# Two self-attentions with their exponentials taken head by head

## What is computed

```
scores = jnp.einsum('bhqd,bhkd->bhqk', q, k) / jnp.sqrt(HEAD_DIM)
scores = jnp.where(causal, scores, -jnp.inf)      # layer 2
attn = jax.nn.softmax(scores, axis=-1)
out = jnp.einsum('bhqk,bhkd->bhqd', attn, v)
```

## Time and profile before

| | us |
|---|---|
| median of 3 runs | 2552.9 |
| lowest and highest run | 2545.34, 2553.57 |
| profiled execution | 2537.7 |
| its span | 2535.8 |
| exponentials of layer 1, first to last start | 743.5 to 966.0 |
| exponentials of layer 2, first to last start | 1782.1 to 1990.2 |

### The profile page before, as it was taken

One profiled execution on the slowest core, in us unless ns is written; L12 is line 12 of the kernel. 1 busy time (PEld: TensorE's weight loads), 2 busy tenths in 40 slices (PEclk: granted clock), 3 DMA queues, 4 the chain that ended last, 5 costly groups with the idle time before them and its releaser, 6 DMA issues. The chain is left out here.

```text
span 2535.8 us, 36942 instructions
## 1 busy us (share of the span) xinstructions
PE 2066.5 (81%) x12688; PEld 1249.8 (49%) x12688; DVE 1552.3 (61%) x3620; ACT 1175.2 (46%) x2304; POOL 762.3 (30%) x938
## 2 busy tenths in 40 slices
PE   5874996768748888997889889775899898677898
PEld 4663662225612324664444444463334466566755
DVE  5867348989848884555554545354567444745676
ACT  3443437644436664224767666533345422133445
POOL 0420005543331100002655555442644100044213
PEclk8985997988959998998999999876789899698899
DMA  1000000000042200002323322102121000200000
GB/s 46 31 7 1 1 1 6 1 28 27 1 117 47 47 2 1 1 1 89 84 72 80 84 71 72 56 1 46 43 55 31 1 1 18 81 1 1 1 1 18
DMA packets 39034, 80.36 MB, mean 32 GB/s; under 512 B 7392, under 2 KB 21728, under 8 KB 37952
## 3 DMA queue, kind: packets, MB, share of 16 engines
q1 hardware_dynamic: 36384, 75.00, 11.1%
q10 hardware_dynamic: 2464, 2.99, 0.5%
HBM read 51.75 MB, written 7.34 MB: 23 GB/s over the span
## 5 line engine op out<-in xcount | busy, mean ns | idle before, releaser
L740 ACT ACTIVATE spt<-P 128x1024 f32<-128x1024 f32 (+3 forms) x256 | 220.9, 863 | 186.0 <-PE P L594 186.0
L707 DVE TENSOR_REDUCE smf<-P 128x2 f32<-128x1024 f32 (+3 forms) x256 | 254.5, 1020 | 47.4 <-PE P L583 24.1
L2274 PEld LDWEIGHTS P<-W,e_h 128*128 128x128 f32 (+1 forms) x1952 | 214.7, 191 | 45.7 <-issue 36.4
L1094 POOL TENSOR_TENSOR d_e<-d_e,d_rc 128x512 f32<-128x512 f32 (+3 forms) x256 | 179.6, 723 | 174.1 <-DVE d_rc L1000 142.8
L2258 PE MATMUL P<-XT,W 128*128 128x512 f32 x424 | 220.1, 617 | 1.2 <-PEq L230 1.2
L2274 PE MATMUL P<-W,e_h 128*128 128x128 f32 (+1 forms) x1952 | 219.2, 278 | 0.0
L2443 DVE SCALAR_TENSOR_TENSOR X<-P,WE,X 128x128 f32<-128x128 f32 x448 | 126.1, 345 | 131.6 <-PE P L2274 130.4
L1043 ACT ACTIVATE d_e<-d_e,d_mn 128x512 f32<-128x512 f32 (+3 forms) x256 | 141.7, 554 | 130.8 <-DVE d_mn L992 130.4
L2322 ACT ACTIVATE e_g<-P 128x512 f32<-128x512 f32 x148 | 88.4, 597 | 240.8 <-PE P L2258 235.3
L2341 DVE TENSOR_TENSOR e_h<-e_g,P 128x512 f32<-128x512 f32 x148 | 101.1, 685 | 108.8 <-PE P L2262 108.5
L2262 PE MATMUL P<-XT,W 128*128 128x512 f32 x296 | 155.8, 608 | 1.6 <-DVE e_h L2341 1.5
(11 more groups left out here) (390 smaller groups left out, 4154.4 us busy)
## 6 DMA issues: line engine op xcount, KB each, us to landing
d_bt<-in_alibi SPq DMA_DIRECT2D x32, 512.0 KB, 3.8
d_moved<-d_raw SPq DMA_DIRECT2D x256, 64.0 KB, 2.4
ska<-parts_k SPq DMA_DIRECT2D x72, 64.0 KB
sqa<-parts_q SPq DMA_DIRECT2D x72, 64.0 KB
W<-in_w_L_xattn SPq DMA_DIRECT2D x1, 4291.0 KB, 12.9
W<-in_w_L_ffn SPq DMA_DIRECT2D x1, 3333.0 KB, 11.1
W<-in_w_L_ffn SPq DMA_DIRECT2D x1, 3155.0 KB, 10.5
parts_k<-sparts SPq DMA_DIRECT2D x8, 384.0 KB, 2.3
```

The source lines that it names most:

```text
L707: v.tensor_reduce(MF[:, n % 2, u, :], P[:, bank:bank + 2, 0:wide(u)], AX.X, ALU.max, negate=True).then_inc(s("max"), 1)
L740: a.activation(PT[:, n % 3, :, t, N - late(t):N], P[:, BANK_T:BANK_T + 2, 0:late(t)], ACT.Exp, scale=SC).then_inc(s("exp"), 1)
L1094: last = g.tensor_tensor(e, e, RC[:, n % 2, u, h:h + 1].to_broadcast([128, 128 * (u + 1)]), ALU.mult)
L2274: last = pe.matmul(P[:, PY + j % 4, 128 * t:128 * (t + 1)], HT[rows, q % RING, blk, 128 * t:128 * (t + 1)], w2, start=n == 0, stop=n == le ...
```

## The change

Exponentials, transposed scores and plain scores are issued for one head at a time. On PE a step is now: transposed scores of head 0, plain scores of head 1, transposed scores of head 1, plain scores of head 0, in layer 2 the two mask products, then the other uses, then `values`. The transposed scores of a head wait only for the exponentials of the same head of the step before. ACT takes 512 columns (in layer 2 up to 512) of one head in an instruction where it took both heads. The counts of the semaphores `score`, `score_t` and `exp` double. The maxima stay one instruction for both heads.

```diff
@@ SyncE
-                    sp.wait_ge(s("score_t"), QT * PAIRS * (b - 1))
+                    sp.wait_ge(s("score_t"), 2 * QT * PAIRS * (b - 1))
@@ TensorE
-            def scores(n, u):
+            def scores(n, u, h):
...
+                r = slice(64 * h, 64 * h + ROWS)
+                last = pe.matmul(P[:, BANK_S + 2 * (c % 2) + h, 0:wide(u)], QA[r, b % 2, p, 128 * u:128 * (u + 1)], KA[r, b % 2, p, 0:wide(u)],
+                                 start=True, stop=not causal)
+                if not causal:
+                    last.then_inc(s("score"), 1)
+
+            def masked(n, u):
+                c = QT * n + u
+                if c == 0:
+                    pe.wait_ge(s("mask"), 1)
                 for h in range(2):
...
+                    pe.matmul(P[:, BANK_S + 2 * (c % 2) + h, wide(u) - 128:wide(u)], k.identb[:], MASK[:], start=False, stop=True).then_inc(s("score"), 1)
...
-            def transposed(n, t):
+            def transposed(n, t, h):
...
                 if QT * n + t:
-                    pe.wait_ge(s("exp"), QT * n + t)
-                for h in range(2):
-                    r = slice(64 * h, 64 * h + 64)
-                    last = pe.matmul(P[:, BANK_T + h, 0:late(t)], KA[r, b % 2, p, 128 * t:128 * (t + 1)], QA[r, b % 2, p, N - late(t):N],
-                                     start=True, stop=True)
-                last.then_inc(s("score_t"), 1)
+                    pe.wait_ge(s("exp"), 2 * (QT * n + t - 1) + h + 1)
+                r = slice(64 * h, 64 * h + 64)
+                pe.matmul(P[:, BANK_T + h, 0:late(t)], KA[r, b % 2, p, 128 * t:128 * (t + 1)], QA[r, b % 2, p, N - late(t):N],
+                          start=True, stop=True).then_inc(s("score_t"), 1)
...
                 for u in range(QT):
-                    if 0 <= n - 2 < ITEMS:
-                        transposed(n - 2, u)
+                    for h in range(2):
+                        if 0 <= n - 2 < ITEMS:
+                            transposed(n - 2, u, h)
+                        if n < ITEMS:
+                            scores(n, u, 1 - h)
+                    if causal and n < ITEMS:
+                        masked(n, u)
                     for what, which in step_uses(n, u):
                         other(what, which)
-                    if n < ITEMS:
-                        scores(n, u)
@@ VectorE
-                v.wait_ge(s("score"), c + 1)
+                v.wait_ge(s("score"), 2 * (c + 1))
@@ ScalarE
-                a.wait_ge(s("score_t"), QT * n + t + 1)
                 if n >= 3:
                     a.wait_ge(s("value"), QT * ((n - 3) // 2) + t + 1)
-                a.activation(PT[:, n % 3, :, t, N - late(t):N], P[:, BANK_T:BANK_T + 2, 0:late(t)], ACT.Exp, scale=SC).then_inc(s("exp"), 1)
+                for h in range(2):
+                    a.wait_ge(s("score_t"), 2 * (QT * n + t) + h + 1)
+                    a.activation(PT[:, n % 3, h, t, N - late(t):N], P[:, BANK_T + h, 0:late(t)], ACT.Exp, scale=SC).then_inc(s("exp"), 1)
@@ GpSimd
-                g.wait_ge(s("exp"), QT * n + t + 1)
+                g.wait_ge(s("exp"), 2 * (QT * n + t + 1))
```

More of the change, by code:

```diff
@@ L574, in scores @@
                     pe.wait_ge(s("max"), c - 1)
-                for h in range(2):
[L576 to L581, removed]
-                    for h in range(2):
-                        last = pe.matmul(P[:, BANK_S + 2 * (c % 2) + h, wide(u) - 128:wide(u)], k.identb[:], MASK[:], start=False, stop=True)
-                last.then_inc(s("score"), 1)
-            def transposed(n, t):
+                r = slice(64 * h, 64 * h + ROWS)
[7 more added lines that the diff above has]
+                    pe.wait_ge(s("mask"), 1)
+                for h in range(2):
+                    pe.matmul(P[:, BANK_S + 2 * (c % 2) + h, wide(u) - 128:wide(u)], k.identb[:], MASK[:], start=False, stop=True).then_inc(s("score"), 1)
+            def transposed(n, t, h):
                 b, p = n // PAIRS, n % PAIRS
@@ L606, in values @@
                 if half == 0:
-                    pe.wait_ge(s("kept" if causal else "exp"), QT * (2 * g + 1) + t + 1)
+                    if causal:
+                        pe.wait_ge(s("kept"), QT * (2 * g + 1) + t + 1)
+                    else:
+                        pe.wait_ge(s("exp"), 2 * (QT * (2 * g + 1) + t + 1))
                 cols = slice(N - late(t) + late(t) // 2 * half, N - late(t) + late(t) // 2 * (half + 1))
```

## The result

The changed kernel takes 2528.49 us (median of 4 runs, 2524.45 to 2532.89), the kernel before 2552.65 in the runs beside it: ratio 0.9911, with a 95% interval of 0.9886 to 0.9937. That is 24 us, 0.9%. The profiled execution of the changed kernel took 2532.89 us with a span of 2530.9, while that of before had 2537.7. So the one pair of traces differs by 4.8 us and the medians by 24. Both numbers need explaining.

A forecast was written before the change was run, and what follows sets the result against it. Layer 1 was taken as bound by the PE-ACT round trip of 1.51 to 1.55 us, layer 2 by a nearly full PE. Layer 1 -9.3 and layer 2 -5.8 give 2522.6 profiled; plus 15.2, 2538 (2522 to 2559).

The forecast's parts named there:

- The loop of layer 1: Plain groups of layer 1: the longest loop takes 2.46 us for two steps, eight steps 11.65 against 12.81.
- the counts, put at 0: PE's 512 extra semaphore increments were taken to cost nothing; by a 26 ns rule they would be an estimated 13 us.
- Groups with k or q: Layer 1 groups with a k or q projection: maxima behind its cast delay plain scores; 13.5 us against 13.57, nothing gained.
- With v: Layer 1's two groups with a v projection, which ACT takes out: 12.75 us against 13.6, -0.86 each.
- with a result: Layer 1's three groups with "turned" and "result": exponentials and maxima come later; 15.45 us against 14.81, +0.64 each.
- Head and tail: Ends of layer 1: -2.5 us at the head, partly at half clock, and -2.1 in eight steps without plain scores.
- The groups between: Layer 1's groups between head and tail: plain -4.6, k or q -0.3, v -1.7, result +1.9, sum -4.7 us.
- Layer 2: Layer 2, PE nearly full: eight plain steps 10.14 us against 10.73; with all groups, head and tail -5.8 us.
- a fall of the clock in layer 2: Layer 2: a falling clock was named as something that would show the prediction wrong; no size given.
- B, the gain eaten by late other uses: Rival, chance 0.27: late maxima and "turned" cost 24 groups about 0.6 us more each; -1 us in all, 2552.
- A, DVE less late: Rival, chance 0.14: DVE's slack covers its lateness, so k, q and result groups gain too; -30 us, 2523.
- C, products that don't overlap: Rival, chance 0.10: transposed beside plain scores on PE don't overlap, +0.8 us in each of 32 groups; +20, 2573.

The follow-up runs named there:

- e1_counts: The kernel before with only the change's extra semaphore increments on PE (512 more) and the waits doubled to match: 2551.11 us, ratio 1.0023.
- e4_others_between: The changed kernel with the other uses of a step moved between the two heads, in both layers: 2542.98 us, ratio 0.9985 to the kernel before.
- e5_mixed: The changed kernel with other uses between the two heads in layer 1 only, layer 2 as in the change: 2521.02 us, ratio 0.9880 to the kernel before.
- b1_before_again: The kernel before, profiled a second time with nothing changed: 2555.56 us, layer 2's block 280.6 us.
- e7_layer1_only: Layer 1 changed with other uses between the two heads, layer 2 word for word as in the kernel before: 2539.45 us, ratio 0.9943 to that kernel.
- e2_order: The changed kernel's order, but one exponential for both heads as in the kernel before: 2567.25 us, ratio 1.0077 to the kernel before.
- e3_split: The change's exponentials by single heads, but in the order of the kernel before: 2553.27 us, ratio 1.0011 to the kernel before.

## Why the prediction was right, and where it was not

The time forecast was 2538 with 2522 to 2559; it is 2528.5, and faster by more than 0.3% was the likeliest case. The gain forecast was 15 us. The medians gained 24.2, just outside the forecast's own band of 8 to 22, and the blocks of the two first profiles 13.4, against a sum of 15.1. So the mechanism came out as worked out, and that the total of the medians lies in the range is in part luck: it holds some 10 us that the prediction did not see coming.

*The loop of layer 1.* Right. Two steps were worked out at 2.46 and take 2.52; eight plain steps at 11.65 and take 11.83 to 11.93. A third to a half of the rest can be the counts, put at 0: 0.09 by e1_counts, in the kernel before.
*Groups with k or q.* Right: 13.5 worked out, 13.6 to 13.7 measured (13.57 before), nothing gained. With v 12.75 against 12.92, with a result 15.45 against 15.39. That the other uses behind the scores are the cause was shown by e4_others_between, where they fall to 12.96, 12.27 and 14.30.
*Head and tail.* Worked out at -2.5 and -2.1, they are -3.5 (up to the first copy) and -1.0. The groups between are -3.0 where the sum had -4.7. Layer 1 in all: -7.5 us against -9.3.
*Layer 2.* -5.9 against -5.8 when the two first traces are compared, and 9.93 for eight plain steps against 10.14. That the sum agrees is luck, since its terms do not. Four plain groups gave -3.2 and the two with v +2.5, where -3.6 was worked out for the six; k and q -1.1 against -1.2; results +0.4 against 0; head and tail -4.6 against -1.4. The groups with v depend on the clock, in the changed kernel too: 14.5 and 14.4, where the same code took 11.50 once in e5_mixed. The prediction named a fall of the clock in layer 2 as a sign of being wrong. It did fall (0.94 where it had 1.00), and the block was faster all the same.
*B, the gain eaten by late other uses:* false; in layer 1 the groups named pay what was worked out, and no more. *A, DVE less late:* false for the change, though the time measured lies between its 2523 and the forecast; e4_others_between shows that there was more to be had, 9.3 us.
*C, products that don't overlap:* false. They start 0.01 apart in layer 1, and products of different widths in layer 2 can do so too:

```profile
1943.38 0.39 PE L595 MATMUL P<-sqa,ska 64*128 64x512 bf16 x1
1943.39 0.23 PE L576 MATMUL P<-ska,sqa 48*128 48x128 bf16 x1
1943.45 0.38 PE L595 MATMUL P<-sqa,ska 64*128 64x512 bf16 x1
```

**The step that failed** is in the end of the sum: "The median of the runs shown lies 15.2 above the profiled one, so I predict 2538." I carried that gap over as if it were the same for both kernels, but the changed kernel's profile lies 4.4 above its median. The first profile of before was quick in two ways. Layer 2's attention had its short form, 269.9 us, where the long form has 280.6, 10.7 more. And the rest of the program took 1988.3 us, where b1_before_again took 7.0 more and the changed kernel 8.5 more. The changed kernel showed 264.0 and 263.7 for layer 2 in two profiles, and its ten timed runs lie within 2524.45 to 2532.89. Against the long form the change gains 16.7 us in layer 2 and 7.5 in layer 1: 24.2, the difference of the medians. So exact an agreement is chance, since the rest of the program varies by more than that.

How often before has the long form is inferred. Of four profiles of that code of layer 2 (three of the kernel before, and e7_layer1_only) two had it. For the runs without a profile of their own only the mean granted clock is known; it was 0.886 in both long profiles and 0.892 to 0.895 in the short ones of the kernel before. Of the 17 runs of before beside e5_mixed, five took 2538.22 to 2545.42 us at 0.892 to 0.895, and twelve 2553.07 to 2560.28 at 0.883 to 0.889, with none between. The ten of e7_layer1_only part likewise, three at 2529.89 to 2531.83 us and seven at 2538.62 to 2543.08. The changed kernel's ten have 0.890 to 0.895. That fits two forms, of which the long one is the commoner. But a long run isn't always the long form: e1_counts took 2553.47 with layer 2 at 270.3, by the rest of the program.

Why the change escapes the long form is argued, not shown. It does not remove the cause: its wait for POOL is longer (1.27 against 0.80), and the clock falls after it too. But its clock was low for the same stretches in both profiles, and never for the 23.9 us in a row that the long form of before shows behind 1850. The order seems to matter more than the split: the order alone (e2_order) had layer 2 at 263.6 us, the split alone (e3_split) had the long form, 280.3. Those are one profile each; the mean granted clock of their timed runs, 0.893 to 0.896 and 0.887 to 0.890, points the same way.

## What to carry to other kernels

An engine with one buffer that goes round (product, function, product) was sped up here by splitting the work in two only when something else could run beside the half that waits; in layer 1, splitting alone gained nothing and reordering alone lost 27 us. Work that another engine waits for belongs into the wait that a split opens, not behind it, but only where there is such a wait. And one profiled execution is not the median: before a gap between the two is carried over to another kernel, take the profile again and ask which stretch of it can have two lengths: look at the granted clock where TensorE waits for a slow queue.

## What the hardware showed that I had not expected

After waits of TensorE of 0.70 to 1.27 us for GpSimd, in stretches where it was otherwise nearly full (8.7 to 9.6 us busy in the 10 us ahead of the waits), the granted clock fell to its lower level, mostly 0.1 to 2.1 us behind the wait, in some executions and not in others with the same wait (0.80 in both pairs of rows above). With that wait gone it stayed at 1.00 from 1820 to 1960 us, in two kernels. Waits of 0.61 to 0.77 us for ScalarE and VectorE, in the profiles of the change between 1860 and 1980 us, were not followed by a fall. Each semaphore increment more on TensorE cost about 6 ns (0.09 us for 16, e1_counts). Two products in different halves of the array, 64 rows and 48 rows, start 0.01 us apart also when they belong to different groups of work.
